# The ramp from self-attention to cross-attention in one fused transformer block, its steps put in another order on three engines

## Chip, cores and metric

The kernel runs on 1 core of one Trainium2 chip. The metric is the time of one execution in device microseconds (us), and the median of several executions is compared. Engines: PE is TensorE (PEld its weight loads), DVE is VectorE, ACT is ScalarE, POOL is GpSimd, SP is SyncE, which issues most transfers. Each engine works through its own queue in program order and waits on semaphores.

## What is computed

One block of a diffusion transformer in float32: self-attention, cross-attention over a context, and a feed-forward part, each with its layer norm and a residual sum. The input has 8 batches of 256 tokens of width 128; the context has 8 times 1601 tokens of width 96; there are 16 heads of width 64.

```python
attn_in = _adaln(x, cond, ln1_w, ln1_b, g1_w, g1_b, b1_w, b1_b)
x = _attn(attn_in, attn_in, sa_wq, sa_wkv, sa_wo, sa_bo) + x
cross_in = _adaln(x, cond, ln1_w, ln1_b, g1_w, g1_b, b1_w, b1_b)
ctx_n = _ln(context, ca_lnc_w, ca_lnc_b)
x = _attn(cross_in, ctx_n, ca_wq, ca_wkv, ca_wo, ca_bo) + x
ffn_in = _adaln(x, cond, ln2_w, ln2_b, g2_w, g2_b, b2_w, b2_b)
h = jax.nn.gelu(ffn_in @ ff_w1 + ff_b1, approximate=False)
x = h @ ff_w2 + ff_b2 + x
```

`_attn` projects q, k and v, rotates q and k (rotary embedding), takes the softmax of the scaled scores, multiplies by v and projects back.

## The kernel before

Each attention is a loop of 64 steps, one for each batch and pair of heads. Every engine runs its own order of short words; a word is a step function with a number and, after a plus, how many steps ahead of the loop it works (`k2+1` is chunk 2 of the keys of the next step). The functions hold the waits, so an order only decides what stands in front of what in an engine's queue; the waits decide when it runs.

A cross-attention step on PE:

- `k0` to `k3` (L1322) project the keys in four chunks of 512, 512, 512 and 65 into two alternating banks, and `q` (L1307) projects the queries. `v0` to `v3` (L1335) project the values into the one bank that `q`, the softmax sums and the output also use.
- `a0` to `a6` (L1354) are scores for the row maximum, in halves of 1024 scores a row pair. They have one bank pair, `MP`, so `a(n+1)` waits until DVE has reduced `a(n)` with `am(n)` (L1068). `a0` also waits for `qh`.
- `s0` to `s6` (L1373) are the scores proper, in one other bank pair, `SP`; `s(n+1)` waits for the exponentials `e(n)` on ACT (L851). `p0` to `p6` (L1387) are the products with the values.

DVE turns the keys out of the bank (`kt`, L1033), multiplies by the cosines (`kc`, L1039), adds the half that SP's transfer has swapped (`ka`, L1046), and takes the low part (`kl`, L1054) after ACT took the high part (`kh`). The queries take the same way with `qt` and `qc` (L1017, L1023) on DVE, a swap by SP, the sum on POOL (L685) and `qh` on ACT (the function `copy`, L728). ACT also reads the values out of their bank (`ve`, L728), and starts the transfer of the maxima (`mr`, L382).

The ramp stands between the last step of self-attention (its steps have a `z` in front: `zsum`, `zp`, `zo`, `zrc`, `zdv`, `zad`) and the steady loop. In it three more things must be done: the rest of cross step 0 that comes before its scores; the start of step 1; and a layer norm over the three chunks of x that are new (batches 2 to 7), called `LN2`. The norm goes through PE, DVE and ACT by turns: `mean` (L1126), `centre` on DVE (L922), `square` on ACT (L735), `var` (L1134, 4 matmuls of one column), `root` on ACT (L740, for all three chunks, behind the load of another function table and with a load back after it), `inverse` on DVE (L928), `spread` (L1144, 4 matmuls of 128 columns), `unit` on DVE (L932), `out` on ACT (L747). `mean` and `spread` write into `SP`, the bank pair of the scores, so `s0` comes after all of them. `q+1` reads what `out0` wrote.

The three orders of the ramp are written out by hand; a word of the loop that stands in the ramp is left out of the loop. They are `RAMP` for PE (L1151), and `ramp` for DVE (L1100) and for ACT (L868). SP and POOL have no order of their own that the change touches.

Of the kernel before, what the change touches and what calls it, by code (L numbers as in the profile page):

```python
# [65 lines left out]
def block_kernel(nc, xT_in, cT_in, ctx_in, cols_in, cols96_in, ada_in, packs, w1_in, w2_in,  # L66
# [34 lines left out]
    with ExitStack() as ctx:  # L101
# [210 lines left out]
        def run_steps(a, body, last=True):  # L312

            for j in range(-a.lead, STEPS + (a.lag if last else 0)):
                body(j)
# [9 lines left out]
        def wait(eng, semaphore, value):  # L325

            if value > 0:
                eng.wait_ge(semaphore, value)
# [8 lines left out]
        def in_order(order, do, ahead=()):  # L337

            def body(j):
                for what, k, by in order:  # L340
                    if 0 <= j + by < STEPS and (what, k, j + by) not in ahead:
                        do[what](j + by, k)
            return body
# [51 lines left out]
        def run_words(order, *tables):  # L395

            for text in order.split():
                what, k, _ = Stage.word(text)
                [table[what] for table in tables if what in table][0](k)

        def last_step(words):

            def run(J, k):
                if J == STEPS - 1:
                    run_words(words[1][k], *words[0])
            return run

        def of(do, J):
            return {w: (lambda k, w=w: do[w](J, k)) for w in do}

        def run_ramp(order, do, *tables):

            for text in order.split():
                what, k, J = Stage.word(text)
                if what in do:
                    do[what](J, k)
                else:
                    run_words(what + str(k), *tables)

        def ahead(*orders):  # L420
            return [(what, k, J) for order in orders for what, k, J in map(Stage.word, order.split())]

        def last_self(do):
            return {"z" + w: (lambda k, w=w: do[w](STEPS - 1, k)) for w in do}
# [301 lines left out]
        def _(act):  # L726
# [3 lines left out]
            def norm(ln, by=""):  # L730

                def square(k):
                    wait(act, ln.centred, k + 1)
                    wait(act, ln.var, k - 1)
                    act.activation(ln.sq[k % 2][:, :], ln.xc[k][:, :], ACT.Square).then_inc(ln.squared, 1)  # L735

                def root(g):
                    columns = ln.columns(g)
                    wait(act, ln.var, ln.groups[g][-1] + 1)
                    act.activation(lnsd_[:, columns], ln.var_bank[:, columns], ACT.Sqrt, bias=epsc[:, :]  # L740
                                   ).then_inc(ln.std, 1)

                def affine(k):
                    wait(act, ln.unit, k + 1)
                    for h in range(2):
                        b = 2 * ln.chunks[k] + h
                        ins = act.activation(ainT[:, b * N:(b + 1) * N], ln.xc[k][:, h * N:(h + 1) * N],  # L747
                                             ACT.Identity, scale=mod[:, 2 * ln.i, b:b + 1],
                                             bias=mod[:, 2 * ln.i + 1, b:b + 1])
                    ins.then_inc(ln.done, 1)  # L750

                return {by + "square": square, by + "root": root, by + "out": affine}
# [109 lines left out]
            def cross(do):  # L862

                do["n"] = last_step(([norm(LN3)], ["square0 square1", "square2", "root0"]))
                def table(k):
                    act.activation(warm[:, 1 + k:2 + k], epsc[:, :], (ACT.Sqrt, ACT.Exp)[k])

                ramp = ("table0 square0 kh2 square1 kh3 ve0 square2 ve1 root0 mr table1 out0 out1 kh0+1 out2 qh+1 e0 ve2 "  # L868
                        "e1 kh1+1 e2 ve3")
                run_ramp(ramp, do, norm(LN2), {"table": table})  # L870
                run_steps(a_, in_order(a_.act, do, ahead(*RAMP_ACT.values(), ramp)), False)

                def gelu(n):
                    f = n % FF
                    act.wait_ge(s_h, n + 1)
                    if n == 0:
                        act.wait_ge(x.kl, NK * STEPS)
                    wait(act, s_f, n - 3)
                    act.activation(hidden_sb[n % 4], hidden_bank[n % 3][:, :], ACT.Gelu, bias=cols[:, 12 + f:13 + f]
                                   ).then_inc(s_g, 1)  # L880

                run_words("e1 e2 e3 ve3 out0 e4 out1 e5 out2 e6 g0 g1 oe0 g2 g3 g4 g5 g6 g7 bsquare0 g8 broot0 g9 g10 g11 bout0 "
                          "g12 g13 g14 g15", of(do, STEPS - 1), norm(LN3), norm(LNL, "b"), {"g": gelu})
# [11 lines left out]
            act.wait_ge(s_rows, 5)  # L895
            self_attention(do)
            cross(do)


        @block.vector  # L900
        def _(dve):
# [16 lines left out]
            def norm(ln, by=""):  # L918

                def centre(k):  # L920
                    wait(dve, ln.mean, k + 1)
                    dve.tensor_tensor(ln.xc[k][:, :], ln.x(k), ln.mean_bank[k % len(ln.mean_bank)][:, :], ALU.subtract  # L922
                                      ).then_inc(ln.centred, 1)

                def inverse(g):
                    columns = ln.columns(g)
                    wait(dve, ln.std, g + 1)
                    dve.reciprocal(lnrstd_[:, columns], lnsd_[:, columns]).then_inc(ln.inv, 1)  # L928

                def unit(k):  # L930
                    wait(dve, ln.cast, k + 1)
                    dve.tensor_tensor(ln.xc[k][:, :], ln.xc[k][:, :], ln.spread_bank[k % len(ln.spread_bank)][:, :], ALU.mult  # L932
                                      ).then_inc(ln.unit, 1)

                return {by + "centre": centre, by + "inverse": inverse, by + "unit": unit}

            def add_to_x(x_b, bank, bias):

                if bias is None:
                    return dve.tensor_tensor(x_b, x_b, bank, ALU.add)  # L940
                return dve.scalar_tensor_tensor(out=x_b, in0=bank, scalar=cols[:, bias:bias + 1], in1=x_b,
                                                op0=ALU.add, op1=ALU.add)
# [154 lines left out]
            def cross(do, words):  # L1097

                do["n"] = last_step(([norm(LN3)], ["centre0", "centre1 centre2"]))
                ramp = ("am0 zrc zdv am1 kl1 am2 centre0 ka2 centre1 kt3 kc3 kl2 am3 zad centre2 ka3 am4 kl3 kt0+1 am5 "  # L1100
                        "kc0+1 am6 nm inverse0 unit0 unit1 kt1+1 unit2")
                run_ramp(ramp, do, last_self(words), norm(LN2))
                run_steps(a_, in_order(a_.dve, do, ahead(*RAMP_DVE.values(), ramp)), False)

                def add_ff(c):
                    dve.wait_ge(s_f, (c + 1) * FF)
                    add_to_x(xT[:, c * LNC:(c + 1) * LNC], ff_out[c], 10).then_inc(s_y, 1)

                run_words("inverse unit0 unit1 unit2 rc0 dv0 ad0 y0 bcentre0 binverse0 y1 bunit0 y2 y3",
                          of(do, STEPS - 1), norm(LN3), norm(LNL, "b"), {"y": add_ff})  # L1110
# [10 lines left out]
        def _(pe):  # L1121
            def norm(ln, by=""):
# [15 lines left out]
                def spread(k):  # L1138
# [9 lines left out]

                return {by + "mean": mean, by + "var": variance, by + "spread": spread}

            RAMP = ("a0 zsum0 zp0 a1 mean0 mean1 k3 a2 zo0 a3 var0 a4 k0+1 var1 mean2 v0 a5 v1 var2 a6 spread0 spread1 "  # L1151
                    "k1+1 spread2 q+1 s0 v2 s1 p0 s2 p1 v3")

            def x_uses(a, first=()):

                names = [w[0] for w in a.xuses]
                uses = [w for w in first if w[0] in names and w[0::2] != ("q", 0)]
                for j in range(-a.lead, STEPS + a.lag):
                    uses += [(w, k, j + by) for w, k, by in a.xuses
                             if 0 <= j + by < STEPS and (w, k, j + by) not in first]  # L1160
                return uses
# [124 lines left out]
            def cross_words():  # L1286

                uses = x_uses(a_, ahead(*RAMP_PE.values(), RAMP))

# [123 lines left out]
            def cross(do, words):  # L1413
# [16 lines left out]

                run_ramp(RAMP, do, last_self(words), {"mean": ramp_mean, "var": ramp_variance, "spread": ramp_spread})
                chunks_mean = norm(LN3)
# [6 lines left out]
                def variance(k):  # L1439
# [5 lines left out]
                                     ["mean0", "mean1", "mean2 var0", "var1", "var2"]))  # L1445
                run_steps(a_, in_order(a_.pe, do, ahead(*RAMP_PE.values(), RAMP)), False)

# [111 lines left out]
```

## Time and profile before

| what | value |
|---|---|
| median of 3 executions | 1942.67 us (1939.44 to 1943.04) |
| the profiled execution, its own time | 1940.06 us |
| span of that execution, first to last instruction | 1938.3 us |
| PE busy | 1886.2 us (97%) |
| DVE, ACT, POOL busy | 1573.7, 945.6, 1266.3 us |
| where the ramp lies | about 403 to 458 us from the span's start |

The span is the time between the first and the last instruction on the core; the 1.8 us around it are the same for any order of the ramp. PE is busy nearly throughout, at 2.4 GHz when the granted clock reads 1.00 and at 1.2 GHz when it reads 0.50. Outside the ramp and the first 45 us the clock is at 1.00.

### The profile page before, as it was taken

How to read it: one execution, taken by the hardware profiler on the slowest of the kernel's cores; microseconds unless marked ns; L12 is line 12 of the kernel's file. 1: busy time of each engine (PE TensorE's matmuls, PEld its weight loads, DVE VectorE, ACT ScalarE, POOL GpSimd, SP SyncE). 2: the span in 40 equal slices, each digit the busy share in tenths (PEclk: the TensorE clock that was granted, in tenths of full speed). 3: DMA queues.
4: the chain of work that ended last, by engine and by line, in shares of the span. 5: the costliest groups of instructions: out<-in, count | busy, mean ns of one | idle time of the engine just before them, and what ended most of it. 6: DMA issues, size and time to landing. Idle time of an engine off the chain costs nothing.

```text
span 1938.3 us, 52005 instructions
## 1 busy us (share of the span) xinstructions
PE 1886.2 (97%) x19952; PEld 1288.5 (66%) x19952; DVE 1573.7 (81%) x2292; ACT 945.6 (49%) x1460; POOL 1266.3 (65%) x816
## 2 busy tenths in 40 slices
PE   7989999988999999999999999999999999999999
PEld 5656766755666666666666666666666666666664
DVE  5998888867888888888888888888888888888852
ACT  3445554533544544444554444445544445554444
POOL 5777756415677667666766766776676676767652
PEclk9999999978999999999999999999999999999999
DMA  6322233201111111111111111111111111111110
GB/s 189 105 80 85 78 107 90 78 30 49 59 52 56 51 55 50 56 57 54 56 51 54 52 56 56 54 55 52 53 53 56 56 55 53 54 51 54 50 32 23
DMA packets 147729, 119.07 MB, mean 61 GB/s; under 512 B 63392, under 2 KB 111648, under 8 KB 147488
## 3 DMA queue, kind: packets, MB, share of 16 engines
q1 hardware_dynamic: 110624, 115.46, 17.9%
q10 hardware_dynamic: 36864, 0.28, 1.0%
q8 instruction: 166, 2.72, 0.6%
q14 instruction: 75, 0.61, 0.1%
HBM read 36.71 MB, written 1.05 MB: 19 GB/s over the span
## 4 chain that ended last, share of the span: by engine, by line
PE 86%; issue 3%; DVE 3%; DMA 3%; POOL 2%; SPq 1%; ACT 1%; ACTq 0%; DVEq 0%; POOLq 0%
PE S L1373 24%; PE OB L1387 20%; PE PB L1335 10%; PE PB L1322 9%; PE S L1354 7%; DMA swapped<-turned 2%; PE PB L1396 2%; PE PB L1307 2%; PE S L1224 2%; PE PB L1406 1%; PE PB L1270 1%; PE OB L1252 1%; PE OB L1235 1%; PE PB L1190 1%; DVE QK L966 1%
## 5 line engine op out<-in xcount | busy, mean ns | idle before, releaser
L708 POOL TENSOR_TENSOR psum_acc<-psum_acc,P 124x1024 f32<-124x1024 f32 (+1 forms) x320 | 689.8, 2156 | 214.7 <-ACT P L851 205.2
L851 ACT ACTIVATE P<-S 124x1024 f32<-124x1024 f32 (+1 forms) x448 | 431.3, 963 | 512.4 <-PE S L1373 512.3
L1068 DVE TENSOR_REDUCE mxc<-S 128x2 f32<-128x1024 f32 x384 | 470.0, 1224 | 91.4 <-PE S L1354 84.4
L1387 PE MATMUL OB<-P,V 124*64 124x256 f32 (+1 forms) x3328 | 436.0, 386 | 0.0
L1387 PEld LDWEIGHTS OB<-P,V 124*64 124x64 f32 (+1 forms) x3328 | 221.0, 136 | 187.6 <-issue 103.4
L701 POOL TENSOR_TENSOR psum_acc<-P 124x1024 f32<-124x1024 f32 x64 | 152.0, 2375 | 211.8 <-ACT P L851 208.3
L1373 PE MATMUL S<-QH,KH 64*124 64x256 f32 (+1 forms) x1664 | 272.0, 323 | 5.8 <-ACT P L851 5.8
L728 ACT ACTIVATE V<-PB 124x512 f32<-124x512 f32 (+1 forms) x320 | 157.2, 491 | 203.0 <-PE PB L1335 165.3
L1373 PEld LDWEIGHTS S<-QH,KH 64*124 64x124 f32 (+1 forms) x1664 | 154.1, 181 | 128.2 <-issue 104.3
L1373 PE MATMUL S<-QL,KH 64*124 64x256 f32 (+1 forms) x1664 | 235.1, 278 | 0.0
L1373 PE MATMUL S<-QH,KL 64*124 64x256 f32 (+1 forms) x1664 | 234.8, 278 | 0.0
L1373 PE MATMUL S<-MX,share 64*124 64x256 f32 (+1 forms) x1664 | 234.7, 278 | 0.0
L1335 PE MATMUL PB<-kv_w,ctxT_all 96*64 96x128 f32 (+2 forms) x3328 | 230.4, 276 | 0.4 <-DVE qrot L1023 0.4
L1322 PE MATMUL PB<-ctxT_all,kv_w 96*64 96x512 f32 (+1 forms) x1024 | 221.4, 510 | 0.2 <-issue 0.2
L1335 PEld LDWEIGHTS PB<-kv_w,ctxT_all 96*64 96x64 f32 (+2 forms) x3328 | 187.5, 135 | 37.1 <-issue 17.7
L1033 DVE TENSOR_TENSOR turned<-PB,rope 128x512 f32<-128x512 f32 (+1 forms) x256 | 145.4, 568 | 73.3 <-PE PB L1322 73.3
L1354 PE MATMUL S<-KH,QH 64*128 64x512 f32 (+1 forms) x1024 | 189.1, 386 | 7.6 <-DVE mxc L1068 4.8
L1046 DVE TENSOR_TENSOR PB<-PB,swapped 128x512 f32<-128x512 f32 (+1 forms) x256 | 147.8, 577 | 17.0 <-DMA swapped<-turned 14.4
L728 ACT ACTIVATE KH<-PB 128x512 fp32r<-128x512 f32 (+1 forms) x256 | 128.6, 502 | 65.5 <-DVE PB L1046 61.8
L1373 PEld LDWEIGHTS S<-QH,KL 64*124 64x124 f32 (+1 forms) x1664 | 155.2, 183 | 3.0
L1373 PEld LDWEIGHTS S<-MX,share 64*124 64x124 f32 (+1 forms) x1664 | 155.1, 182 | 0.0
L1373 PEld LDWEIGHTS S<-QL,KH 64*124 64x124 f32 (+1 forms) x1664 | 154.4, 182 | 0.0
(159 smaller groups left out, 2828.7 us busy)
## 6 DMA issues: line engine op xcount, KB each, us to landing
swapped<-turned SPq DMA_DIRECT2D x512, 128.0 KB, 2.1
kv_w<-sa_kv_dram SPq DMA_DIRECT2D x64, 128.0 KB, 2.3
qswapped<-qturned SPq DMA_DIRECT2D x128, 64.0 KB, 1.9
kv_w<-ca_kv_dram SPq DMA_DIRECT2D x64, 96.0 KB, 2.2
ctxT_all<-ctx_dram SPq DMA_DIRECT2D x8, 624.0 KB, 4.6
q_w<-sa_wq_dram SPq DMA_DIRECT2D x64, 64.0 KB, 2.0
q_w<-ca_wq_dram SPq DMA_DIRECT2D x64, 64.0 KB, 1.9
o_w<-ca_wo_dram SPq DMA_DIRECT2D x64, 64.0 KB, 2.0
```

The source lines that it names most:

```text
L701: pool.tensor_tensor(acc, P_of(J, 0)[0:rows], P_of(J, 1)[0:rows], ALU.add).then_inc(x.acc, 2)
L708: pool.tensor_tensor(acc, acc, P_of(J, c)[0:rows, :, 0:w], ALU.add).then_inc(x.acc, 1)
L728: return act.activation(out, in_, ACT.Copy)
L851: act.activation(P_of(J, c)[0:rows, :, 0:w], SP[0:rows, :, 0:w], ACT.Exp, scale=SCALE).then_inc(x.e, 1)
L1033: dve.tensor_tensor(turned[c][:, 0:w], KB[c % 2][:, 0:w], rope[:, M + lo:M + lo + w], ALU.mult).then_inc(x.kt, 1)
L1046: dve.tensor_tensor(KB[c % 2][:, 0:w], KB[c % 2][:, 0:w], swapped[c][:, 0:w], ALU.add).then_inc(x.ka, 1)
L1068: dve.tensor_reduce(mxc[:, t, :, c:c + 1], MP[:, :, 0:w], AX.X, ALU.max).then_inc(x.am, 1)
L1322: ins = pe.matmul(KB[c % 2][half(h), 0:w], kv_w[J % UNROLL][0:DC, half(h)], ctxT_all[0:DC, at:at + w], start=True, stop=True)
L1335: ins = pe.matmul(XB[a:b, k * PAIR:(k + 1) * PAIR], ctxT_all[0:DC, lo + a:lo + b], kv_w[J % UNROLL][0:DC, PAIR:2 * PAIR], start=True, stop ...
L1354: ins = pe.matmul(MP[:, h, at:at + w], QH[J % UNROLL][half(h), t::2], KH[J % 2][half(h), lo:lo + w], start=True, stop=True)
L1373: ins = pe.matmul(SP[0:w, h, k * N:(k + 1) * N], keys[half(h)], queries[half(h), :], start=(n == 0), stop=(n == len(terms) - 1))
L1387: ins = pe.matmul(OB[half(h), 0:N], Vb[J % 2][0:w, t, half(h)], P_of(J, c)[0:w, h, k * N:(k + 1) * N], start=(t == 0), stop=(t == len(a_.t ...
```

## The change

Three strings are rewritten; nothing is computed otherwise, and no instruction is added or dropped.

```diff
@@ ACT, the ramp
-                ramp = ("table0 square0 kh2 square1 kh3 ve0 square2 ve1 root0 mr table1 out0 out1 kh0+1 out2 qh+1 e0 ve2 "
-                        "e1 kh1+1 e2 ve3")
+                ramp = ("kh2 table0 kh3 square0 square1 ve0 mr square2 ve1 root0 table1 ve2 kh0+1 out0 out1 out2 e0 ve3 "
+                        "e1 qh+1 kh1+1 e2")
@@ DVE, the ramp
-                ramp = ("am0 zrc zdv am1 kl1 am2 centre0 ka2 centre1 kt3 kc3 kl2 am3 zad centre2 ka3 am4 kl3 kt0+1 am5 "
-                        "kc0+1 am6 nm inverse0 unit0 unit1 kt1+1 unit2")
+                ramp = ("am0 zrc zdv kl1 am1 ka2 kt3 kc3 am2 am3 ka3 am4 kl2 am5 centre0 kl3 zad am6 nm centre1 kt0+1 centre2 "
+                        "kc0+1 inverse0 unit0 unit1 ka0+1 kt1+1 unit2")
@@ PE, the ramp
-            RAMP = ("a0 zsum0 zp0 a1 mean0 mean1 k3 a2 zo0 a3 var0 a4 k0+1 var1 mean2 v0 a5 v1 var2 a6 spread0 spread1 "
-                    "k1+1 spread2 q+1 s0 v2 s1 p0 s2 p1 v3")
+            RAMP = ("a0 zsum0 zp0 a1 k3 a2 zo0 a3 mean0 mean1 a4 a5 var0 a6 mean2 v0 var1 k0+1 v1 var2 k1+1 v2 "
+                    "spread0 spread1 spread2 s0 v3 q+1 s1 k2+1 p0 a0+1 s2 p1 k3+1 a1+1")
```

Three places show how the queues move. First PE, from the output projection of self-attention (`zo`, the 16 matmuls of L1270) on. Before, `a3`, `var0`, `a4`, `k0+1`, `var1`, `mean2` and the first piece of `v0` followed it:

```order
L1270 MATMUL PB<-oTs,o_w 64x256 x16
L1354 MATMUL S<-KH,QH 128x512 x2
L1134 MATMUL OB<-meanw,QK 128x1 x4
L1354 MATMUL S<-KH,QH 128x512 x2
L1322 MATMUL PB<-ctxT_all,kv_w 64x512 x2
L1134 MATMUL OB<-meanw,QK 128x1 x4
L1126 MATMUL S<-xT,meanw 128x512
L1335 MATMUL PB<-kv_w,ctxT_all 64x128
```

Of the change the rows behind `zo` are `a3`, `mean0 mean1`, `a4 a5`, `var0`, `a6`, `mean2` and the first piece of `v0`:

```order
L1354 MATMUL S<-KH,QH 128x512 x2
L1126 MATMUL S<-xT,meanw 128x512 x2
L1354 MATMUL S<-KH,QH 128x512 x4
L1134 MATMUL OB<-meanw,QK 128x1 x4
L1354 MATMUL S<-KH,QH 128x66 x4
L1126 MATMUL S<-xT,meanw 128x512
L1335 MATMUL PB<-kv_w,ctxT_all 64x128
```

So `a4` and `a5` stand side by side with nothing between them, `var0` stands right behind `a5`, and `k0+1` has moved behind `var1`.

The same place on DVE, from the scaling of self-attention's last output (`zdv`, L982) on. Before, it went `zdv`, `am1`, `kl1`, `am2`, `centre0`, `ka2`, `centre1`:

```order
L982 TENSOR_TENSOR oTs<-oraws,PB 128x256
L1068 TENSOR_REDUCE mxc<-S 128x2
L1054 TENSOR_TENSOR KL<-PB,KH 128x512
L1068 TENSOR_REDUCE mxc<-S 128x2
L922 TENSOR_TENSOR ctree<-xT,S 128x512
L1046 TENSOR_TENSOR PB<-PB,swapped 128x512
L922 TENSOR_TENSOR ctree<-xT,S 128x512
```

Of the change, from `zdv` to `centre0`:

```order
L982 TENSOR_TENSOR oTs<-oraws,PB 128x256
L1054 TENSOR_TENSOR KL<-PB,KH 128x512
L1068 TENSOR_REDUCE mxc<-S 128x2
L1046 TENSOR_TENSOR PB<-PB,swapped 128x512
L1033 TENSOR_TENSOR turned<-PB,rope 128x65
L1039 TENSOR_TENSOR PB<-PB,rope 128x65
L1068 TENSOR_REDUCE mxc<-S 128x2 x2
L1046 TENSOR_TENSOR PB<-PB,swapped 128x65
L1068 TENSOR_REDUCE mxc<-S 128x2
L1054 TENSOR_TENSOR KL<-PB,KH 128x512
L1068 TENSOR_REDUCE mxc<-S 128x2
L922 TENSOR_TENSOR ctree<-xT,S 128x512
```

`kl1` comes ahead of `am1`, and `centre0` has moved from behind `am2` to behind `am5`, the last reduction in these rows.

The third place is ACT from the load back to the exponentials' table (L866) on. Before (`out0 out1`, `kh0+1`, `out2`, `qh+1`, `e0`, `ve2`, `e1`):

```order
L866 ACTIVATE warm<-epsc 128x1
L747 ACTIVATE ainT<-ctree,mod 128x256 x4
L728 ACTIVATE KH<-PB 128x512
L747 ACTIVATE ainT<-P,mod 128x256 x2
L728 ACTIVATE QH<-qrot 128x256
L851 ACTIVATE P<-S 124x1024
L728 ACTIVATE V<-PB 124x512
L851 ACTIVATE P<-S 124x1024
```

Of the change (`ve2`, `kh0+1`, `out0 out1`, `out2`, `e0`, `ve3`, `e1`, `qh+1`):

```order
L866 ACTIVATE warm<-epsc 128x1
L728 ACTIVATE V<-PB 124x512
L728 ACTIVATE KH<-PB 128x512
L747 ACTIVATE ainT<-ctree,mod 128x256 x4
L747 ACTIVATE ainT<-P,mod 128x256 x2
L851 ACTIVATE P<-S 124x1024
L728 ACTIVATE V<-PB 113x128
L851 ACTIVATE P<-S 124x1024
L728 ACTIVATE QH<-qrot 128x256
```

All three `out` now stand behind `kh0+1` and directly ahead of `e0`, and `qh+1` has moved behind `e1`. On PE `q+1` has moved with it, from ahead of `s0` to behind `v3`, whose bank it shares. The queues of POOL and SP are the same.

## Rows read from the trace of the kernel before

**Rows 1.** The page: span, PE's busy time, and its granted clock in 40 slices.

```profile
span 1938.3 us, 52005 instructions
...
PE 1886.2 (97%) x19952; PEld 1288.5 (66%) x19952; DVE 1573.7 (81%) x2292; ACT 945.6 (49%) x1460; POOL 1266.3 (65%) x816
...
PEclk9999999978999999999999999999999999999999
```

**Rows 2.** Windows: length, busy time (instructions) of PE, PEld, DVE, ACT, POOL; granted clock; DMA.

```profile
403.50:406.90 3.40, 3.40 (x16) 1.53 (x14) 2.92 (x3) 0.48 (x2) 0.29 (x1) 0.50 0.21 77
407.00:417.00 10.00, 9.41 (x62) 5.07 (x60) 7.62 (x12) 3.11 (x5) 0.00 (x0) 1.00 0.08 21
417.20:434.00 16.80, 15.61 (x74) 11.06 (x74) 6.62 (x12) 5.81 (x11) 0.00 (x0) 0.50 0.05 16
434.20:441.00 6.80, 3.88 (x44) 2.95 (x44) 4.62 (x8) 2.93 (x6) 1.45 (x2) 1.00 0.19 68
441.00:444.30 3.30, 3.18 (x22) 2.56 (x24) 0.00 (x0) 1.54 (x3) 0.00 (x0) 0.51 0.00 0
444.50:451.20 6.70, 4.39 (x40) 2.40 (x36) 3.05 (x4) 1.53 (x3) 4.61 (x2) 1.00 0.11 42
451.40:458.00 6.60, 4.99 (x26) 2.69 (x26) 5.19 (x8) 0.82 (x2) 0.00 (x0) 0.50 0.11 30
458.00:470.00 12.00, 12.00 (x128) 7.95 (x128) 10.14 (x18) 5.34 (x8) 8.93 (x5) 1.00 0.22 73
```

**Rows 3.** Timeline of PE, ramp's first part: start, length, instruction, idle before it.

```profile
403.08 0.51 PE L1354 MATMUL S<-KH,QH 64*128 64x512 f32 x2 [2.87 <-issue]
...
406.99 1.98 PE L1126 MATMUL S<-xT,meanw 128*128 128x512 f32 x4
...
409.83 3.67 PE L1270 MATMUL PB<-oTs,o_w 128*64 128x256 f32 x32
...
416.81 1.59 PE L1134 MATMUL OB<-meanw,QK 128*128 128x1 f32 x8
...
423.18 1.97 PE L1335 MATMUL PB<-kv_w,ctxT_all 96*64 96x128 f32 x16
...
428.46 3.75 PE L1144 MATMUL S<-ident,lnrstd 128*128 128x128 f32 x16 [0.95 <-DVE lnrstd L928]
...
432.15 1.98 PE L1322 MATMUL PB<-ctxT_all,kv_w 96*64 96x512 f32 x4
```

**Rows 4.** Timeline from q+1 to a4 of step 1, PE and ACT.

```profile
435.21 0.65 PE L1307 MATMUL PB<-ainT,q_w 128*64 128x256 f32 x4
...
435.79 0.38 PE L1373 MATMUL S<-QH,KH 64*124 64x256 f32 x2
...
439.64 0.42 ACT L728 ACTIVATE QH<-qrot 128x256 fp32r<-128x256 f32 x1 [1.09 <-POOL qrot L685]
439.97 1.00 ACT L851 ACTIVATE P<-S 124x1024 f32<-124x1024 f32 x1
...
448.00 0.50 PE L1354 MATMUL S<-KH,QH 64*128 64x512 f32 x2
...
458.33 0.51 PE L1354 MATMUL S<-KH,QH 64*128 64x512 f32 x2
```

**Rows 5.** Timeline of DVE and ACT: am1, centre0, square0, a table load, out2.

```profile
407.21 1.22 DVE L1068 TENSOR_REDUCE mxc<-S 128x2 f32<-128x1024 f32 x1
...
411.08 0.68 DVE L922 TENSOR_TENSOR ctree<-xT,S 128x512 f32<-128x512 f32 x1
...
411.79 0.63 ACT L735 ACTIVATE QK<-ctree 128x512 f32<-128x512 f32 x1 [3.50 <-DVE ctree L922]
...
429.38 1.28 ACT L866 ACT_TABLE_LOAD   x1 [2.13 <-issue]
...
437.47 1.08 ACT L747 ACTIVATE ainT<-P,mod 128x256 f32<-128x256 f32 x2
```

**Rows 6.** The page, issues of transfers: KB each, us from issue to landing.

```profile
swapped<-turned SPq DMA_DIRECT2D x512, 128.0 KB, 2.1
```

## The prediction, as it stood before the changed kernel ran

> **What bounds the kernel now.** I read the page first: PE is busy for 1886.2 of 1938.3 us, and its clock is full except in two of forty slices, which hold the ramp [rows 1]. An edit of the ramp happens once, so all it can move is what PE loses there. Then windows cut where the clock changes [rows 2]. From 407 to 417 PE is busy 9.41 of 10 us at full clock. From 417.2 to 434.0 it is busy 15.61 of 16.80 us, but at 1.2 GHz. From 434.2 to 458 it waits much more: 6.80 - 3.88, 3.30 - 3.18, 6.70 - 4.39 and 6.60 - 4.99 make 6.96 us idle, and two of the four stretches run at 1.2 GHz. From 458 on it is busy 12.00 of 12.00 us. So the ramp loses time twice, in its first part by a slow clock over dense work, in its second part by waits; and `a4` of step 1 at 458.33 [rows 4] is the finishing post. Whatever comes earlier or later there, the rest of the span does too, since PE is the bound from there on.
>
> **The prices.** At half clock: a variance product 1.59 us, a `v` group 1.97, a `k` chunk 1.98, a spread 3.75 / 2 = 1.88 (two in the row). At full clock two means took 1.98, so 0.99 each. A `v`, a `k` and a spread I take at half their price at full clock, and a mean at twice its own at half clock (2.0). `zo` is 3.67, an `a` 0.51 [rows 3]. On the others: a maximum 1.22, a centring 0.68 (I take it for `kl`, `ka`, `kc`, `kt` of 512 columns as well), a square 0.63, one `out` 1.08 [rows 5], an exponential 1.00 [rows 4].
>
> **Part 1, up to the first variance product.** All is the same until DVE is free at 407.21 [rows 5] and PE has done `a1` at about 407.0, where its next row begins [rows 3]. Now `kl1` goes first: 407.9; `am1` after it: 407.9 + 1.2 = 409.1. PE had the first two means there; now it stands until 408.0 for `k3` (which needs `kl1`), works 0.3, and stands again for `am1`: `a2` at 409.2. `zo` starts at 409.7, as before 409.83, and ends at 413.4. `a3` and two means: 413.4 + 0.4 + 2.0 = 415.8; the reduction `am3` is hidden under the means. `a4` 415.8 to 416.3, `am4` to 417.5, and only then `a5`, to 418.0: nothing stands between the two, so PE waits 1.2. DVE does `kl2` first (418.2), then `am5` (419.4), `centre0` (420.1), ACT `square0` (420.75). `var0` stands directly behind `a5`, so PE idles from 418.0 to 420.8. Behind that one waiting instruction are queued `a6`, `mean2`, `v0` and all the rest, and `v0` needs nothing of the norm.
>
> What does the clock do with it? It halved at 403.5 behind an idle stretch of 2.87 us [rows 3]. It also halved at 417.2, in a stretch where PE's records are 94% busy [rows 2] with no idle gap near 1 us, but with variance products of one column among them. So I take it as certain that it is at half from about 420. Whether it also halves at 409 to 411, behind the two new gaps of 1.0 and 0.8 us, is about even. The nearest row is the half-clock stretch of 3.4 us at 403.5 [rows 2]; over `zo` it costs 3.4 / 2 = 1.7. `var0` starts at 420.8 or 422.5.
>
> **Part 2, from there to `s0`.** PE has three variance products (4.8), `a6` (0.6, an estimate from an `a` of 66 columns against 0.51 at full clock), one mean (2.0), three `v` (5.9) and two `k` (4.0): 17.3 us at half clock, against none for the waits, except that `centre2` now stands behind `kt0+1`, so after `k0+1` it takes 0.68 + 0.68 + 0.63 = 2.0 until `var2` can run, and `v1` covers 1.97: 0.1 to 0.3, say 0.3. Then three spreads. Before, the clock came back at 434.2, during a dense stretch of spreads and `k1+1` [rows 2, 3]; now `k1+1`, `v2` and the spreads are a dense stretch of their own, so I take it back by then: 3 x 0.94 = 2.8. `s0` starts at 420.8 + 17.6 + 2.8 = 441.2, or at 442.9 with the halved `zo`. Before it was 435.79 [rows 4]. That is 5.4 or 7.1 us late. Of this only `v2` (2.0) and what `q+1` saves (0.6) is work that is moved; the rest is idle time and work at half clock.
>
> **Part 3, from `s0` to `a4`.** Here the new order should do better, since `k2+1`, `a0+1`, `k3+1` and `a1+1` stand among the scores. Step by step from `s0`: the last spread ends there, so `unit1` is just done; `ka0+1` 0.45 later, `kh0+1` (0.6) at 1.05, three `out` x 1.08 to 4.3, `e0` to 5.3, `ve3` to 5.7, and `q+1` can write at 5.8. PE has done `s0` and `v3` by 1.5 and then idles some 4 us, as before it did for `e0` (439.97 - 435.79 = 4.2). From `q+1` to the start of `qh+1` takes 439.64 - 435.21 = 4.43 [rows 4], of which 2.1 is the swap [rows 6]; plus 0.42 for `qh+1`: `a0+1` at 5.8 + 4.9 = 10.7. `s1`, `k2+1` and `p0` lie under it even at half clock (about 5). From `a0+1` to `a4` took 458.33 - 448.00 = 10.33 [rows 4]. It is a chain of reductions on DVE, with `kt3` and its swap in it, and stays one: `am0+1` still stands behind `kt2+1 kc2+1`, and `ka3+1` still waits 2.1 for SP ahead of `am3+1`. I keep 10.3. Together 21.0 to 21.1, against 458.33 - 435.79 = 22.54: a gain of 1.4. Of the bounds, below: were each reduction to follow its `a` at once, it is 4 x (1.22 + 0.51) = 6.9 and the gain is 4.8; above: nothing, were `s1` and `k2+1` late.
>
> **Sum.** 5.4 - 1.4 = +4.0, or 7.1 - 1.4 = +5.7; between them +4.9. Against its own time the profiled execution would read 1940.1 + 4.9 = 1945.0; it stands 2.6 below the median of the runs, and the median would be 1942.7 + 4.9 = 1947.6 us. ACT's moved steps cost nothing extra: `kh2` and the first table load lie under `zo`, and the load back lies under `k1+1` and `v2` (4.0 us at half clock); uncovered, a load is 1.28 us [rows 5]. SP's and POOL's queues keep their order, and no transfer is queued behind a new one.
>
> **The rivals.**
>
> *The clock comes back early*, within `k0+1` and `v1`: then `k0+1`, `v1`, `k1+1` and `v2` save half of 7.9, less the 1.0 that `var2` now really waits for `square2`. That is 3 less than +4.0 to +5.7: +1 to +2.7. For it: four such words are as dense as what stood at 403.5 to 406.9, after which the clock rose. Against it: from 420.2 on, two `v` groups and `a5` filled PE at half clock and it did not rise [rows 2].
>
> *The clock stays full throughout.* Then part 2 is 3 x 1.05 (estimate: two thirds of 1.59) + 0.5 + 1.0 + 3.0 + 2.0 + 1.0 wait + 2.8 = 13.4, `s0` at 420.8 + 13.4 = 434.2 to 434.9, 0.9 to 1.6 early, and the sum is -2.3 to -3.0: no slower, and not far from what can be told from no change. It decides from the point at which PE's idle 2.8 us ahead of `var0` leaves the clock alone. The Trainium skill, "TensorE: Matmul & The Clock Gate", section "Why this matters for your kernels", says that the clock drops between bursts of matmuls behind an idle gap of a certain length, and none of the walk's gaps ahead of `s0` is as long as that, so by that rule the sum would be -2.3. The trace does not agree: the clock halved at 417.2 with no such gap.
>
> *Faster by more.* If beside the full clock `e0` is not held by the three `out` (3 x 1.08 = 3.2), the sum is -2.3 - 3.2 = -5.5. The order on ACT speaks against it, and only an early norm could bring it.
>
> *Half clock right through.* The clock does not come back for the spreads: + 2.8, and `s0`'s and `s1`'s work with it: +8.5 or more. For it speaks that 16.8 us at half clock did not end before PE was dense [rows 2]; against it, that `k1+1`, `v2` and the spreads are longer without a gap than anything there.
>
> *Nothing happens*, because the ramp is not on PE's path: excluded by 12.00 busy of 12.00 behind it.
>
> **How the numbers follow.** What a measurement here can tell from no change is 0.2%, 3.9 us. Main case, half clock from 420 to the spreads, 0.56, with its own range +3 to +7 and three quarters of it above 3.9; early return 0.17; full clock 0.11; faster by more 0.06; half right through 0.10. Slower: 0.42 + 0.10 = 0.52. Faster: 0.06. The same: 0.42. The range leaves out the faster case and the worst of the slow one: 1942.7 - 2.3 = 1940.4 to 1942.7 + 8.5 = 1951.2.
>
> **What would show it.** In the changed kernel's trace: PE idle for 2 to 3 us ahead of the first variance product, released by ACT's square; the clock at 0.50 from about 420 until the norm's spreads; `s0` at 441 to 443; `out`, `out`, `out`, `e0` in a row on ACT with PE idle for about 4 us; `a0+1` some 11 us behind `s0`; `a4` of step 1 at 462 to 464. It would be wrong if the clock stands at 1.00 through the products of the norm, if `var0` finds its square ready, or if `a0+1` to `a4` takes much less than 10 us. The start of the slow clock may lie otherwise from run to run; if so, times of the changed kernel spread more than before.

## The result, and the profile after

| | before | changed |
|---|---|---|
| median | 1941.02 us (1939.44 to 1943.04, 6 runs) | 1948.86 us (1948.33 to 1954.48, 6 runs) |
| profiled execution: span | 1938.3 us | 1946.5 us |

The ratio is 1.0038 with a 95% interval of 1.0025 to 1.0052: the changed kernel is slower, by 7 to 8 us, where +4.9 was predicted. The interval reaches from 4.9 to 10.1 us, so the forecast sum stands at its lower edge. 1948.86 lies inside the range of 1940.4 to 1951.2.

The page of the changed kernel, its span and the clock in 40 slices, against [rows 1]:

```profile
span 1946.5 us, 52005 instructions
...
PEclk9999999988999999999999999999999999999999
```

Windows of the changed kernel, cut where its clock changes. They answer to [rows 2], with the same columns:

```profile
409.60:423.20 13.60, 7.90 (x50) 4.12 (x50) 9.44 (x15) 2.94 (x5) 0.00 (x0) 0.99 0.06 15
423.60:444.00 20.40, 19.97 (x101) 14.82 (x101) 4.01 (x8) 4.70 (x8) 0.00 (x0) 0.50 0.04 14
444.20:450.80 6.60, 2.95 (x33) 2.09 (x33) 2.31 (x5) 4.61 (x9) 0.00 (x0) 1.00 0.11 40
450.90:454.10 3.20, 3.20 (x20) 1.96 (x20) 2.53 (x5) 1.02 (x1) 0.36 (x1) 0.50 0.21 65
454.20:461.30 7.10, 5.52 (x48) 2.97 (x44) 6.49 (x9) 2.53 (x4) 5.70 (x4) 0.98 0.10 38
461.40:464.60 3.20, 3.20 (x22) 2.23 (x20) 2.10 (x6) 0.24 (x2) 0.00 (x0) 0.52 0.22 62
464.60:475.00 10.40, 10.40 (x106) 6.65 (x108) 8.85 (x15) 4.68 (x6) 6.89 (x4) 1.00 0.22 71
```

While the clock was full, PE idled 13.60 - 7.90 = 5.7 us of 13.60 (before, 0.59 of 10); then, when its work came, it did 20.40 us of it at half clock (before, 16.80). The same on the timeline of PE and ACT, start, length, instruction and the idle time before it, against [rows 3 to 5]:

```profile
405.72 0.51 PE L1354 MATMUL S<-KH,QH 64*128 64x512 f32 x2 [3.45 <-issue]
...
410.39 0.34 PE L1322 MATMUL PB<-ctxT_all,kv_w 96*64 96x65 f32 x4 [0.91 <-issue]
...
411.57 0.51 PE L1354 MATMUL S<-KH,QH 64*128 64x512 f32 x2 [0.84 <-DVE mxc L1068]
...
412.01 3.67 PE L1270 MATMUL PB<-oTs,o_w 128*64 128x256 f32 x32
...
419.89 0.51 PE L1354 MATMUL S<-KH,QH 64*128 64x512 f32 x2 [1.41 <-DVE mxc L1068]
...
423.06 1.43 PE L1134 MATMUL OB<-meanw,QK 128*128 128x1 f32 x8 [2.66 <-ACT QK L735]
...
440.18 4.75 PE L1144 MATMUL S<-ident,lnrstd 128*128 128x128 f32 x24
...
444.86 0.38 PE L1373 MATMUL S<-QH,KH 64*124 64x256 f32 x2
...
447.79 1.08 ACT L747 ACTIVATE ainT<-P,mod 128x256 f32<-128x256 f32 x2
448.77 1.01 ACT L851 ACTIVATE P<-S 124x1024 f32<-124x1024 f32 x1
...
450.08 0.65 PE L1307 MATMUL PB<-ainT,q_w 128*64 128x256 f32 x4 [3.65 <-ACT V L728]
...
455.24 0.51 PE L1354 MATMUL S<-KH,QH 64*128 64x512 f32 x2
...
464.49 0.51 PE L1354 MATMUL S<-KH,QH 64*128 64x512 f32 x2
```

The waits stand where they were forecast: 0.91 ahead of `k3`, 0.84 ahead of `a2`, 1.41 ahead of `a5`, 2.66 ahead of `var0` with ACT's square as the releaser, 3.65 ahead of `q+1`.

One caution on this pair of profiles. The spans differ by 8.2 us, but `a0` of step 0, ahead of which nothing was changed, starts 405.72 - 403.08 = 2.6 later. Over the 14 profiles of this study it starts at 403.1 to 409.0, whatever the ramp. So I measure the ramp itself by the interval from that `a0` to `a4` of step 1, behind which PE is dense: 458.33 - 403.08 = 55.3 before, 464.49 - 405.72 = 58.8 after.

Two limits of this measure. Of the 8.2 us, 2.6 lie ahead of `a0`, 3.5 in the interval, and the last 2.1 behind `a4`. Over the 14 profiles that last part takes 1479.9 to 1482.7 us. The clock is not at 1.00 everywhere outside the ramp: before, it is at 0.50 from 1885.0 to 1888.2, and in the changed kernel from 1891.4 to 1898.0, near the end of the kernel, which nothing here changes. And in nine of the 14 profiles a half-clock stretch that began in the interval goes on behind `a4`, for 0.9 to 4.0 us (in the first ones of before and of the changed kernel it does not). The interval leaves out what that costs, up to 2 us, so a difference of less than 2 us between intervals shows nothing.

### The profile page after: what moved, and what is told of

Its sections match the earlier page's. It is cut to its first block, busy times and chain, and to the rows that moved or that the text cites. A ratio compares the mean times of both kernels' runs of the same rounds, so it can differ in the third digit from the quotient of the medians.

```text
span 1946.5 us, 52005 instructions
## 1 busy us (share of the span) xinstructions
PE 1887.9 (97%) x19952; PEld 1289.5 (66%) x19952; DVE 1573.9 (81%) x2292; ACT 946.2 (49%) x1460; POOL 1267.2 (65%) x816
## 3 DMA queue, kind: packets, MB, share of 16 engines
HBM read 36.71 MB, written 1.05 MB: 19 GB/s over the span
## 4 chain that ended last, share of the span: by engine, by line
PE 86%; DVE 3%; issue 3%; DMA 3%; POOL 2%; SPq 1%; ACT 1%; ACTq 0%; DVEq 0%; POOLq 0%
PE S L1373 24%; PE OB L1387 20%; PE PB L1335 10%; PE PB L1322 9%; PE S L1354 7%; DMA swapped<-turned 3%; PE PB L1307 2%; PE PB L1396 2%; PE S L1224 1%; PE PB L1406 1%; PE PB L1270 1%; PE OB L1235 1%; PE OB L1252 1%; DVE QK L966 1%; PE PB L1190 1%
```

## The experiments

The median of before was 1942.9, 1942.7 and 1943.8 us in the three sets of runs (23, 31 and 24 runs), and 1941.0 in the set of the result; each ratio is against before in the same set. The interval and the two columns behind it are read from one profile of each row. "zo" is the time from `a2` to `a3`, in which the output projection lies; "half" is the half-clock time between `a3` and the end of the spreads, read in steps of 0.5 us.

| kernel | ratio to before (95%) | a0 to a4 | zo | half |
|---|---|---|---|---|
| before | 1 | 55.3 | 4.0 | 17 |
| changed | 1.0038 (1.0025 to 1.0052) | 58.8 | 4.0 | 20.5 |
| e1_again | 1.0043 (1.0030 to 1.0056) | 63.1 | 6.7 | 24 |
| e2_early_only | 1.0046 (1.0033 to 1.0059) | 63.9 | 5.7 | 20.5 |
| e3_late_only | 0.9988 (0.9977 to 1.0000) | 50.3 | 4.0 | 10 |
| e4_fill_gap | 1.0046 (1.0032 to 1.0060) | 62.1 | 6.7 | 24 |
| e5_means_back | 1.0033 (1.0022 to 1.0043) | 60.1 | 4.1 | 24 |
| e6_centre_early | 1.0029 (1.0017 to 1.0041) | 61.2 | 6.9 | 20.5 |
| e7_k0_in_gap | 1.0034 (1.0022 to 1.0045) | 61.9 | 6.6 | 20.5 |
| e8_tail_best | 0.9984 (0.9970 to 0.9998) | 47.6 | 4.0 | 3.5 |
| e9_mended | 1.0004 (0.9992 to 1.0015) | 54.4 | 4.0 | 13.5 |
| e10_short_var | 1.0015 (1.0003 to 1.0027) | 55.0 | 6.6 | 7 |
| e11_best | 0.9961 (0.9944 to 0.9978) | 48.5 | 4.0 | 13.5 |
| e12_before_again | one profile | 51.6 | 4.0 | 3.5 |

The theory to be tested: the new order's first part costs, by waits of PE and by work at half clock, and its tail gains. The rival: the tail costs (three `out` ahead of `e0`, `q+1` late), and the first part is harmless.

**e1_again**, the changed kernel unchanged.

> The changed kernel once more. From a0 of step 0 to a4 of step 1 before took 55.3 us and the changed kernel 58.8, 3.5 more, while the spans differ by 8.2. If the order of the ramp is the whole cause, the interval stays at 58 to 60 us, and the profile again shows the other 4.7 us. If those come from what self-attention and the last step do from run to run, a0 lies somewhere between 403 and 407 us this time, and the ratio over many rounds is 1.002 to 1.003 and not 1.004. PE should again stand about 2.7 us ahead of the first variance product.

1952.04 us, ratio 1.0043; interval 63.1, above what was expected. The new thing is on PE's timeline:

```profile
410.90 0.79 PE L1351 MATMUL S<-KH,QH 64*128 64x512 f32 x2
412.83 0.48 PE L1319 MATMUL PB<-ctxT_all,kv_w 96*64 96x65 f32 x4 [1.13 <-issue]
414.00 0.80 PE L1351 MATMUL S<-KH,QH 64*128 64x512 f32 x2 [0.69 <-DVE mxc L1067]
414.73 6.00 PE L1267 MATMUL PB<-oTs,o_w 128*64 128x256 f32 x32
```

`zo` takes 6.00 us and not 3.67. (The experiments' line numbers are a few lower, as their orders stand on one line each.) The guess that the order is worth less than the spans' difference was wrong: with `a0` set aside, this profile is slower still than the first. `a0` itself started at 408.2, later than expected.

**e2_early_only** and **e3_late_only**, one half of the change each. For e2 PE's order is the new one up to `var2` and then the old one:

```diff
-... v1 var2 k1+1 v2 spread0 spread1 spread2 s0 v3 q+1 s1 k2+1 p0 a0+1 s2 p1 k3+1 a1+1
+... v1 var2 spread0 spread1 k1+1 spread2 q+1 s0 v2 s1 p0 s2 p1 v3
```

and for e3 the old one up to `a6` and then the new one:

```diff
-... var2 a6 spread0 spread1 k1+1 spread2 q+1 s0 v2 s1 p0 s2 p1 v3
+... var2 a6 k1+1 v2 spread0 spread1 spread2 s0 v3 q+1 s1 k2+1 p0 a0+1 s2 p1 k3+1 a1+1
```

with DVE and ACT cut at the same place.

> The new order only up to the last variance product, the old one from the spreads on. By my account the first part costs 6.4 us up to s0 (less the 2.0 of v2, which now comes after s0 again, so s0 is some 4 to 5 late) and gets none of the 2.9 back: the interval from a0 to a4 is 60 to 62 us, and the kernel 5 us or more slower than before. The rival, that the new tail with its three out ahead of e0 is what costs, says that this kernel is no slower than before: interval 55 to 56.

> The old order up to a6, the new one from there. By my account the tail alone gains up to 2.9 us less what q+1 behind v3 costs: interval from a0 to a4 53 to 55 us, the kernel 0 to 2 us faster than before. The rival that the tail costs says 57 or more and slower by 2 us.

The first part alone gives 1.0046 and the tail alone 0.9988. The rival falls: the tail gains some 2 us (its interval just touches no change), and the first part costs 9. The two add up to 1.0034, which lies within the interval of the whole. Both ratios are about as expected; the intervals from `a0` to `a4` are not: 63.9 where 60 to 62 was expected, and 50.3 where 53 to 55 was.

**e4_fill_gap**, the wait ahead of `var0` filled with work that changes nothing.

```diff
-... a4 a5 var0 a6 ...
+... a4 a5 fill0 var0 a6 ...
+def fill(_):
+    wait(pe, x.w[1], 32)
+    wait(pe, x.kl, 3)
+    for n in range(2):
+        for h in range(2):
+            pe.matmul(KB[0][half(h), 0:512], kv_w[1][0:DC, half(h)], ctxT_all[0:DC, 0:512], start=True, stop=True)
```

> The changed kernel, with k0+1 computed twice beforehand between a5 and var0 (8 matmul records whose results are overwritten later by the same values), so that PE works 1.9 of the 2.7 us in which it waits for the first square. If the idle stretch is what brings the half clock, the clock stays full at least through var0, a6, mean2 and v0 and s0 comes 2 to 4 us earlier: interval 55 to 57. If the variance products of one column and the lack of dense work bring it anyway, as they did before at 417, the clock halves within 3 to 7 us behind the filling and the interval stays within 1.5 us of 58.8. It can't be slower by more than 0.5, since the filling lies in a wait.

1.0046, interval 62.1. Windows of it:

```profile
417.00:423.00 6.00, 4.50 (x20) 1.79 (x18) 3.62 (x5) 0.23 (x1) 0.00 (x0) 1.00 0.01 1
423.50:447.00 23.50, 23.07 (x110) 16.24 (x107) 5.56 (x13) 5.33 (x9) 0.00 (x0) 0.50 0.04 12
```

The filling closes the wait (PE works from 422.6 to 425.5), the half clock begins at about 423.3, inside it, and lasts 23.5 us over records that are 98% busy. So the idle 2.7 us are neither needed for the fall nor what keeps the clock at half, and busy records do not free it. Of the two cases expected the second came, though the clock fell inside the filling and not 3 to 7 us behind it, and the interval lies 3.3 above 58.8 and not within 1.5. The rule of an idle gap that the prediction cites from the Trainium skill ("TensorE: Matmul & The Clock Gate", section "Why this matters for your kernels") does not describe this stretch: PE's longest gap between `a0` and the fall is 1.42 us here.

**e5_means_back**, **e6_centre_early**, **e7_k0_in_gap**: one repair each of the changed kernel, the first and third on PE, the second on DVE.

```diff
e5 -a1 k3 a2 zo0 a3 mean0 mean1 a4
e5 +a1 mean0 mean1 k3 a2 zo0 a3 a4
e6 -am2 am3 ka3 am4 kl2 am5 centre0 kl3
e6 +am2 am3 ka3 centre0 am4 kl2 am5 kl3
e7 -a5 var0 a6 mean2 v0 var1 k0+1 v1
e7 +a5 k0+1 var0 a6 mean2 v0 var1 v1
```

> The changed kernel with the first two means put back ahead of k3, where they fill PE's two waits for DVE. In the changed kernel's second profile the output projection zo took 6.0 us at half clock, where before, with the means ahead of k3, it took 3.67 at full. If those waits are what brings or keeps the half clock over zo, it takes 3.7 again, and the interval from a0 to a4 (58.8 and 63.1 us in the two profiles) falls by 2 to 4 us below their mean, the kernel's median by 3 us against the changed one. The rival, that the place of zo against the clock is chance, says that the interval and the median stay within 1.5 us, since the means' 2 us only change places.

> The changed kernel with centre0 on DVE moved from behind am5 to ahead of am4, so that square0 is done when PE comes to var0. The wait of 2.7 us ahead of var0 should fall to nothing, at a cost of 0.7 us ahead of a5. If the serial chain a5, am5, centre0, square0, var0 is what costs in the first part, the interval falls by about 2 us and the median with it. If PE's work at half clock behind it is the only cost, and it starts earlier but is as slow, the gain is the same 2 us; if the chain is bound elsewhere (centre2 behind kt0+1), the gain is under 1 us.

> The changed kernel with k0+1 moved into the gap between a5 and var0: the same filling as the copies of e4_fill_gap, but of work that must be done anyway. PE then has 2 us less behind the gap, and centre2 no longer waits for k0+1. Expected: s0 2 us earlier, interval and median 2 us shorter than the changed kernel's. If filling the gap gains nothing because the clock takes it back, as the copies gained nothing, the difference is under 0.7 us.

With the means back, PE's timeline in e5 reads

```profile
408.29 2.77 PE L1124 MATMUL S<-xT,meanw 128*128 128x512 f32 x4
410.99 0.34 PE L1319 MATMUL PB<-ctxT_all,kv_w 96*64 96x65 f32 x4
411.69 3.67 PE L1267 MATMUL PB<-oTs,o_w 128*64 128x256 f32 x32
```

The wait ahead of `k3` is gone and `zo` is back at 3.67. This is not chance of one profile: from `a2` to `a3` it is 4.0 to 4.1 us in all seven profiles with the means ahead of `k3`, and 5.7 to 6.9 in six of the seven with `k3` first (the first profile of the changed kernel is the seventh). But a wait of 1.42 us has come ahead of `a4`, where the means stood, and the interval of 60.1 is only 0.9 below the mean of the changed kernel's two, 60.95. In e6 `var0` follows `a5` without its wait. The cost expected ahead of `a5` did not come: that wait is 1.42 where the changed kernel has 1.41, since DVE had idle time ahead of `am4`. Only `a6` now waits a little:

```profile
421.71 0.51 PE L1351 MATMUL S<-KH,QH 64*128 64x512 f32 x2 [1.42 <-DVE mxc L1067]
422.15 1.05 PE L1132 MATMUL OB<-meanw,QK 128*128 128x1 f32 x8
423.64 0.64 PE L1351 MATMUL S<-KH,QH 64*128 64x66 f32 x4 [0.43 <-DVE mxc L1067]
```

From `a3` to `s0` it takes 26.9 us in e6 and 27.2 in e7, against 29.3 and 30.0 in the two profiles of the changed kernel and 30.2 in e4. So an earlier `centre0` (e6) and useful work in the gap (e7) each gain 2 to 3 us there, copies of work gain none. Over the whole interval, 61.2 and 61.9, the 2 us that were expected are not seen. The medians moved by less than expected, 1.0033, 1.0029 and 1.0034 against 1.0038 and 1.0043, and no one of these intervals stands clear of those: one by one the repairs are inconclusive in time.

**e9_mended**, the three repairs in one kernel.

> The changed kernel with all three repairs: the two means back ahead of k3, centre0 ahead of am4, and k0+1 between a5 and var0. If the losses are separate (zo at half clock 2.9 us in most runs, the wait ahead of var0 2.7 us, k0+1 as filling in what is left of it), the interval from a0 to a4 comes to 56 to 58 us and the kernel to 2 to 4 us above before. If one long serial chain through the norm is all, the second and third repair gain nothing beside the first: interval 60 us as in e5_means_back, 1948 us.

1.0004, clear below the changed kernel's 1.0038: the three repairs together take back some 7 us, and the kernel stands 0.8 us above before, where 2 to 4 us were expected to stay. Its new tail gains some 2 us (e3), so by these numbers the mended first part still costs an estimated 3 us; PE still waits 1.41 us ahead of `a4` and again ahead of `a5`. Interval 54.4. The clock no longer stays at half in one piece:

```profile
423.00:429.50 6.50, 6.50 (x30) 3.95 (x28) 3.94 (x9) 0.63 (x1) 0.00 (x0) 0.50 0.02 6
430.00:432.50 2.50, 2.44 (x30) 2.21 (x29) 0.00 (x0) 1.66 (x3) 0.00 (x0) 1.00 0.20 53
433.00:439.50 6.50, 6.50 (x34) 4.91 (x35) 0.92 (x2) 2.35 (x4) 0.00 (x0) 0.50 0.00 0
```

**e10_short_var**: do the variance products hold the clock down? Each variance product of this norm is one matmul of four columns and not four of one; the variances of three of four groups of tokens are left out and the fourth's stands for them. (The edit holds for this norm alone; its condition is left out here.)

```diff
-for t in range(GROUP):
-    ins = pe.matmul(ln.var_bank[:, at + t:at + t + 1], ln.sq[k % 2][:, t * D:(t + 1) * D], meanw[:, 0:1], ...)
+for t in (3,):
+    ins = pe.matmul(ln.var_bank[:, at:at + GROUP], ln.sq[k % 2][:, t * D:(t + 1) * D], meanw[:, 0:GROUP], ...)
```

> The changed kernel, where each of the three variance products of this norm is one matmul instead of four; it leaves out the variances of three of four groups of tokens and uses the fourth's. PE's work shrinks by three quarters of 3 x 1.6 us at half clock, 3.6 us. If the variance products, busy in the records but thin, are what holds the clock at half through this stretch, then without them the mean, v and k work is dense and the clock comes back within some 7 us: half-clock stretch of 3 to 10 us instead of 20.5 to 24, interval 6 us or more below the changed kernel's 58.8 to 63.1. If it is the v and k matmuls themselves that do not bring it back, the stretch stays at 17 to 20 us and the interval falls by about 3.6 us or less.

```profile
423.40:429.90 6.50, 5.00 (x25) 3.11 (x25) 2.42 (x7) 1.26 (x2) 0.00 (x0) 0.50 0.00 0
430.30:443.30 13.00, 8.65 (x86) 6.48 (x86) 5.29 (x9) 8.07 (x15) 0.00 (x0) 1.00 0.12 42
```

The half clock lasts 7 us and not 20.5 to 24, though PE waits for `var0` as before (2.66 us) and its gap ahead of the third product is 1.27. The interval is 55.0, 3.8 and 8.2 below the changed kernel's two, and a half-clock stretch goes on for 4.0 us behind it. The median, 1.0015, is 2.5 thousandths below the mean of the changed kernel's 1.0038 and 1.0043, so 4.9 us. The work left out is 3.8 to 4.3 us of that at half clock (5.1 and 5.6 us of products in the changed kernel's two profiles, 1.3 here). What is left over is less than the intervals of the ratios can tell from nothing, so the times do not show a gain by the clock; the trace shows the shorter stretch, in one profile.

How far does this reach? The products do not start the half clock. In seven of the nine profiles with the new first part, repaired or not, the clock falls ahead of the first product, as in e5, where PE does nothing in between:

```profile
416.00:420.10 4.10, 1.02 (x4) 0.45 (x4) 3.44 (x5) 0.23 (x1) 0.00 (x0) 1.00 0.01 2
420.40:422.20 1.80, 0.00 (x0) 0.00 (x0) 1.63 (x4) 0.63 (x1) 0.00 (x0) 0.50 0.00 0
```

(In the changed kernel's first profile it falls during `var0`, in e6 right behind it.) And all twelve matmuls can run at full clock: in e3, e8 and e12, with the old first part, each product takes 1.05 us. In e9, with all twelve in place, the clock came back between the first and the second product. So e10 speaks for the products as what lengthens a half-clock stretch that has begun; it does not make them the cause of it, and without a second profile it does not settle the matter.

**e8_tail_best** and **e11_best**: the first part of before, and a tail with the maxima of step 1 early, but `q+1` and the `out` steps where they were.

```diff
before: s0 v2 s1 p0 s2 p1 v3
e8 PE: s0 v2 a0+1 s1 a1+1 k2+1 p0 s2 p1 k3+1 v3
e8 DVE, at the end: qt+1 ka0+1 qc+1 kl0+1 kc1+1 ka1+1 am0+1 kt2+1 kc2+1 am1+1 kl1+1
e11 PE: s0 v2 a0+1 s1 a1+1 k2+1 p0 a2+1 s2 k3+1 p1 a3+1 v3 s3 k0+2
e11 DVE: ... am0+1 am1+1 kl1+1 kt2+1 kc2+1 kt3+1 am2+1 kc3+1 ka2+1 am3+1 kl2+1 ka3+1 kl3+1
e11 ACT, at the end: kh2+1 e3 kh3+1
```

> The kernel before with its first part and its q+1 and out steps as they are, and only a0+1, a1+1, k2+1 and k3+1 brought forward on PE, am0+1 and am1+1 with them on DVE. PE idles 2.6 us ahead of s1 before, and 2.3 and 1.6 us between a0+1, a1+1 and a2+1. If the gain of the new tail (s0 to a4 19.6 to 21.1 us, against 22.5) comes from the early maxima and not from the later q+1 and the out steps in a row, this kernel has s0 to a4 in 17 to 19 us and is 3 to 5 us faster than before. If it comes from k1+1 and v2 ahead of the spreads, it is no better than e3_late_only: 0 to 2 us faster.

> The tail of e8_tail_best carried further: a2+1 ahead of s2, a3+1, s3 and k0+2 in the ramp, reductions on DVE ahead of the key steps where their bank allows. In e8_tail_best a1+1 to a2+1 took 5.6 us and s0 to a4 18.5. If the reductions' chain sets the tail, s0 to a4 comes to 16 to 17.5 us and the kernel to 1.5 us below e8_tail_best. If SP's swaps of k2+1 and k3+1 or the clock set it, it stays at 18 to 19.

e8 reaches 0.9984 and e11 0.9961, 1936.34 us against 1943.83 in its set: e11 beats both kernels, and by more than the 1.5 us below e8 that were expected. From `s0` to `a4` e8 took 451.08 - 432.55 = 18.5 us, inside its expectation, and e11 455.09 - 438.51 = 16.6; before took 22.5 in [rows 4] and 23.9 in e12, the changed kernel 19.6 and 20.7. That `a0+1` can go so early is seen in e11 by its releaser:

```profile
443.04 0.79 PE L1351 MATMUL S<-KH,QH 64*128 64x512 f32 x2 [1.81 <-ACT QH L728]
```

4.5 us behind `s0`, where the changed kernel has it 10.4 behind. Compared by the kernels' medians, e8 gained 3.8 us and e11 7.5.

**e12_before_again**, the kernel before unchanged, one profile.

> The kernel before once more, for a second profile of it: zo 3.7 us at full clock, s0 32 to 34 us behind a0, the half-clock stretch through the norm between 3 and 17 us and well below the 20.5 to 24 of the kernels with the new first part; a0 within 3 us of 403. If the place of the half clock over zo is chance and not the means', zo is at half here, 5 us or more.

Its PE timeline has `zo` at 3.67 although it waited 1.39 ahead of `k3`, and its clock, in windows, is full until 426.4:

```profile
401.70:426.40 24.70, 17.94 (x134) 10.97 (x135) 18.64 (x29) 6.75 (x13) 2.72 (x3) 1.00 0.10 33
426.80:429.90 3.10, 3.10 (x15) 2.19 (x13) 1.38 (x2) 2.62 (x5) 0.00 (x0) 0.50 0.05 1
```

`s0` came 27.6 us behind `a0`, not 32 to 34: the norm's half clock was 3.5 us and not 17, and the three variance products of this kernel ran at full clock, as the last one shows:

```profile
423.61 1.05 PE L1132 MATMUL OB<-meanw,QK 128*128 128x1 f32 x8
```

Which of the two profiles is the usual one can be judged by the mean granted clock of whole executions. It was 0.989 in the profile on which the prediction rested, and 0.989 is also the median of 78 executions of before, which lie at 0.986 to 0.995. It was 0.994 in e12, and one of the 78 reaches that. So the first profile was ordinary by its clock and e12 an unusually good one. The changed kernel's eleven executions lie at 0.985 to 0.989.

The Trainium skill, "TensorE: Matmul & The Clock Gate", section "What's actually happening", says that the point at which the clock rises at a kernel's start varies from run to run, because the monitor that sets it runs freely beside the kernel. Here the clock varies in the middle of the kernel too, 17 and 3.5 us at half in two profiles of one program; that the same monitor is the reason is not shown.

## Why the prediction was right, and where its sizes were off

The forecast was slower, by waits of PE and by work at half clock in the first part, and a smaller gain in the tail. e2, e3 and e9 show that account; three of its terms had the wrong size.

*Part 1, to `var0`: right in its steps.* The walk had `var0` 420.8 - 403.1 = 17.7 us behind `a0`, or 19.4 with `zo` at half clock; measured 423.06 - 405.72 = 17.3, and 428.11 - 408.23 = 19.9 in e1. The wait of 2.8 was 2.66. What was off is the term for `zo`, 1.7 us with a chance of about even, so 0.85 of the +4.9. It came in six of seven profiles with `k3` ahead of the means, and from `a2` to `a3` it cost 1.6 to 2.9 us over 4.0, 2.6 to 2.9 in five of the six. Over the seven that is 2.1 on the mean.

*The clock, `var0` to `s0`: right that it is at half, too short.* The prediction let it come back for the spreads. In the changed kernel it stayed at half for all of `k1+1` and `v2` and until the last spread, 20.4 us, and the three spreads took 4.75, not 2.8. `s0` came 39.1 and 42.5 us behind `a0`; forecast were 38.1 and 39.8. That the clock "is at half from about 420" was right: it fell 17.8 us behind `a0`, which is 420.9 on the time scale of before. Why it fell stays open. The prediction named the idle gap and the variance products. The gap ahead of `var0` is not needed, since e4 filled it and the clock fell all the same; the products are not either, since the clock mostly falls ahead of them. What the nine profiles with the new first part have in common is a wait of 1.4 us ahead of `a5`, which no run takes away. But in before, e3 and e11 the clock fell without it, during the second product or within 0.5 us behind it. That the products lengthen the stretch has e10's one profile for it.

*Part 3, `s0` to `a4`: right in mechanism, mis-sized.* Forecast 21.1, measured 19.6 and 20.7, a gain of 2.9 and 1.9 for 1.4. `q+1` came at 5.2 behind `s0` (forecast 5.8), `a0+1` at 10.4 (10.7), and the maxima behind it took 9.3, not 10.3; in e1 4.9, 10.7 and 10.0.

*The sum.* Forecast were +4.0 to +5.7 for the interval; measured are +3.5 and +7.9 in the two profiles against the prediction's own profile. Up to `s0` they are 6.4 and 9.7 late, for 5.4 or 7.1, and the tail gives 2.9 and 1.9 back. By their medians and ratios the kernels differ by 7 to 9 us. With the measured sizes put in, `zo` 2.1 for 0.85, the spreads 4.9 for 2.8 and the tail's gain 2.4 for 1.4, the +4.9 becomes an estimate of +7.3. So the sum was short mainly because the clock was expected back for the spreads and over `zo`. Part of it was luck all the same: the prediction knew one profile of before. Against the second, whose ramp took 51.6 us and not 55.3, the same order would be 7.2 and 11.6 us slower. How the ramps of before are spread between these two is not known. In seven profiles with the new first part (changed, e1, e2, e4 to e7) the clock is at half for 20.5 to 24 us, with the old one (before, e3, e8, e11, e12) for 3.5 to 17.

*The rivals.* An early return of the clock and a full clock did not occur in any of these seven profiles; in e9 and e10 the return did. "Half clock right through", at +8.5 or more, is what the two traces of the changed kernel show, and the medians lie between it and the main case, though it had 0.10. Not settled is why the copies in e4 did nothing where `k0+1` itself in the same gap (e7) gained: less work behind the gap is enough to explain it, but the clock was not held apart. The intervals in time of e5, e6 and e7 do not divide the 9 us among the repairs either.

## What to carry to other kernels

Where several short stretches of a ramp wait on one another, ask of each wait what stands behind it in PE's queue and could stand ahead. e11 gained 7.5 us by maxima that had no reason to come late; the changed order lost about as much although its tail was the better one. Count a wait twice where dense work is queued behind it: in this ramp the work that came behind the new waits ran at half clock, for 20.5 to 24 us. And read more than one profile before a difference of 0.3% is explained, with an interval between two events that bound the edit beside the span; one profile of each kernel would here have given +3.5 us for a change that costs 7 to 9.

## What the runs showed of the hardware

The clock stayed at 1.2 GHz over 23.5 us in which the records have PE busy 98% of the time (e4), and over 20.4 us at 98% in the changed kernel; in e10 it was back at 2.4 GHz after 7 us with PE busy only 5.00 of 6.50. So in these traces PE's busy share in the records does not tell at which level the clock stands. The clock also fell with no gap of PE above 1.42 us since `a0` (e4).

Fourteen profiles, in which everything ahead of `a0` is the same, have that `a0` at 403.1 to 409.0 us, a spread of 5.9 us, which is more than most of the differences studied here. Two profiles of one program spent 17 and 3.5 us of the same ramp at half clock.
